# Turning the attention probabilities by VectorE's 32 by 32 blocks and SBUF to SBUF transfers in a decoder megakernel

## What is computed

```python
q = rope(x @ Wq)        # 8 batches, 32 heads, 128 rows, 128
k = rope(ctx @ Wk)      # 8 heads
v = ctx @ Wv            # 8 heads
p = softmax(q @ k.T / sqrt(128) + mask)   # causal in layer 0, the given mask in layer 1
x = layernorm(x + (p @ v) @ Wo)
```

## Time and profile before

| | us |
|---|---|
| three executions | 2656.85, 2662.54, 2663.20 |
| their median | 2662.54 |
| span of the profiled execution (first to last instruction) | 2658.3 |
| busy in it: TensorE, VectorE, ScalarE, GpSimd | 2568.0, 1579.7, 1074.0, 714.2 |

### The profile page before, as it was taken

The page is one execution under the profiler, slowest core; times in us unless marked ns, Lnnn a source line. Parts: engine busy times, 40 slices in busy tenths (PEclk is TensorE's granted clock), DMA queues, the critical chain, the costliest instruction groups (busy, mean ns, idle before and its releaser), DMA issues.

```text
span 2658.3 us, 39957 instructions
## 1 busy us (share of the span) xinstructions
PE 2568.0 (97%) x15160; PEld 1681.2 (63%) x15160; DVE 1579.7 (59%) x2953; ACT 1074.0 (40%) x3270; POOL 714.2 (27%) x695
## 2 busy tenths in 40 slices
PE   8989999999999899999999999999999989999998
PEld 7855676766665676566676766656775554556664
DVE  3487666766646666776666766454556644334465
ACT  0013444444454466244444444613555412324440
POOL 1037334444321100463334443122211221000002
PEclk9999999999999999999999999999999999999999
DMA  8541001111001100101011110010000020000000
GB/s 175 98 129 54 10 35 40 40 40 36 5 16 40 48 2 2 60 32 36 7 38 40 40 40 17 1 72 33 1 2 29 22 72 28 13 0 25 13 1 32
DMA packets 55359, 94.86 MB, mean 36 GB/s; under 512 B 31456, under 2 KB 40096, under 8 KB 49024
## 3 DMA queue, kind: packets, MB, share of 16 engines
q1 hardware_dynamic: 55168, 92.30, 11.7%
HBM read 83.89 MB, written 8.39 MB: 35 GB/s over the span
## 4 chain that ended last, share of the span: by engine, by line
PE 87%; DVE 8%; ACT 2%; POOL 2%; issue 1%; DMA 0%; DVEq 0%; SPq 0%; POOLq 0%
PE banks L687 12%; PE banks L775 11%; PE banks L759 4%; PE banks L834 4%; PE banks L803 4%; PE banks L668 4%; PE banks L303 3%; PE banks L655 3%; PE banks L2028 3%; PE banks L1450 3%; PE banks L1977 3%; PE banks L2282 2%; PE banks L2005 2%; PE banks L2316 2%; PE banks L813 2%; PE banks L2044 2%
## 5 line engine op out<-in xcount | busy, mean ns | idle before, releaser
L161 POOL TENSOR_TENSOR norm_spread<-norm_mv,const 128x1 f32<-128x1 f32 x96 | 20.7, 216 | 1128.2 <-DVE norm_mv L157 1128.2
L880 ACT ACTIVATE E_x<-S_x,sm_x 128x128 f32<-128x128 f32 x512 | 199.2, 390 | 261.8 <-DVE sm_x L1052 260.4
L1112 POOL TENSOR_TENSOR QT<-QT,const 128x512 f32<-128x512 f32 x128 | 171.1, 1337 | 469.6 <-DVE turned L938 469.6
L687 PE MATMUL banks<-xT,weights 128*128 128x512 f32 x512 | 236.1, 595 | 5.8 <-POOL weights L1107 5.8
L1016 DVE TENSOR_TENSOR x<-banks,x 128x256 f32<-128x256 f32 (+1 forms) x288 | 147.3, 511 | 123.7 <-PE banks L775 119.7
L775 PE MATMUL banks<-weights,OT 128*128 128x256 f32 x768 | 189.4, 379 | 0.0
L1114 POOL TENSOR_TENSOR QT<-QT,turned 128x512 f32<-128x512 f32 x128 | 168.9, 1320 | 10.0
L2415 ACT ACTIVATE E_s<-banks,top_s 128x128 f32<-128x128 f32 x512 | 139.3, 383 | 79.2 <-DVE top_s L2512 79.2
L887 ACT ACTIVATE OT<-banks 128x512 f32<-128x512 f32 x128 | 76.5, 597 | 227.1 <-PE banks L834 227.1
L687 PEld LDWEIGHTS banks<-xT,weights 128*128 128x128 f32 x512 | 95.0, 191 | 114.1 <-issue 106.4
L775 PEld LDWEIGHTS banks<-weights,OT 128*128 128x128 f32 x768 | 141.8, 190 | 38.3 <-DVE x L1016 11.7
(11 more groups left out here) (315 smaller groups left out, 5185.0 us busy)
## 6 DMA issues: line engine op xcount, KB each, us to landing
weights<-in_L_xwq SPq DMA_DIRECT2D x16, 1024.0 KB, 4.9
weights<-in_L_xwo SPq DMA_DIRECT2D x16, 1024.0 KB, 4.9
weights<-in_L_xwk SPq DMA_DIRECT2D x16, 256.0 KB, 5.0
weights<-in_L_xwv SPq DMA_DIRECT2D x16, 256.0 KB, 2.6
weights<-in_L_ffn_W_base SPq DMA_DIRECT2D x3, 1024.0 KB, 5.0
weights<-in_L_xwq SPq DMA_DIRECT2D x4, 768.0 KB, 6.8
weights<-in_L_xwo SPq DMA_DIRECT2D x4, 768.0 KB, 6.3
xT<-in_xT SPq DMA_DIRECT2D x4, 512.0 KB, 9.7
```

Source lines behind the costliest of these rows:

```text
L687: mm = PE.matmul(to, left[:, k, head], moving, start=name in ("P1", "P2", "P4", "P5") and k == 0, stop=k == 1, skip_group_check=name in (" ...
L880: ins = AC.activation(e[:, j, :], s[:, j, :], ACT.Exp, bias=sm[:, 0, j:j + 1], scale=1.0, accum_out=sm[:, 1, j:j + 1])
L1112: PO.tensor_tensor(four(to), four(to), spread(cos128, 4), ALU.mult).then_inc(*pool_step.one())
```

## The change

For the first 62 units of each of the two stages (`direct = units - 2`), the four transposes on TensorE and ScalarE's copy of their result are gone. ScalarE writes and scales E in another order: 16 blocks of 32 columns, block j of head h at place (j, h). VectorE turns E in 32 by 32 blocks into a new tile `blocks` (`turn_blocks`), in the step after the unit's own, right after the maxima. SyncE then starts sixteen transfers (`move`): 32 partitions by 128 columns each, quarter i of the partitions of `blocks` to quarter j of those of PT. TensorE waits for all sixteen and reads PT in the order (h, i, c). E has two tiles instead of three. The last two units of each stage go the old way. The weights wq and wo are loaded in four transfers each instead of one, and SyncE's loads are placed between the units' moves, two groups ahead for wk, wq and wv.

```diff
 def load_cross(stage, free):
...
-            for name, here in (("wk", xwk_in), ("wv", xwv_in), ("wq", xwq_in)):
+            for name, here in (("wk", xwk_in), ("wv", xwv_in)):
                 SP.dma_start(views[name], dram[f"{layer}_x{name}"][0]).then_inc(*here.one())
-            SP.dma_start(views["wo"][0], dram[f"{layer}_xwo"][0]).then_inc(*xwo_in[0].one())
+            for k in range(KC):
+                SP.dma_start(views["wq"][:, k, :], dram[f"{layer}_xwq"][0, :, k, :]).then_inc(*xwq_in.one())
+            for k in range(4):
+                SP.dma_start(views["wo"][0][:, k, :], dram[f"{layer}_xwo"][0, :, k, :]).then_inc(*xwo_in[0].one())
...
+            direct = units - 2
...
-                E = [sbuf(f"E{n}_x{stage}", [P, 4, P], scope) for n in range(3)]
+                E = [sbuf(f"E{n}_x{stage}", [P, 4, P], scope) for n in range(2)]
+                blocks = [sbuf(f"blocks{n}_x{stage}", [P, 4, P], scope) for n in range(2)]
...
+                def flat(t):
+                    return t[:, :, :].rearrange("p a n -> p (a n)")
+
+                def head_of(e, h, u):
+
+                    if u < direct:
+                        return flat(e).rearrange("p (j h c) -> p h j c", j=4, h=4)[:, h, :, :]
+                    return e[:, h, :]
...
+                def turned_rows(u):
+
+                    t = PT[u % 2]
+                    return flat(t).rearrange("p (i h c) -> p h i c", i=4, h=4) if u < direct else t[:, :, :]
...
+                    def move(u):
+
+                        SP.wait_ge(*x_blocks(u + 1))
+                        if u >= 2:
+                            SP.wait_ge(*x_mix(u - 1))
+                        for j in range(4):
+                            for i in range(4):
+                                SP.dma_start(flat(PT[u % 2])[32 * j:32 * j + 32, rows_of(i)], flat(blocks[u % 2])[32 * i:32 * i + 32, rows_of(j)]).then_inc(*x_pt_in[u % 2].one())
+
+                    load_keys(1)
+                    load_queries(1, range(KC))
+                    load_values(1)
+                    load_out(1, range(4))
+                    for u in range(direct):
+                        g, b = divmod(u, B)
+                        move(u)
+                        if b == 2 and g + 2 < G8:
+                            load_keys(g + 2)
+                        if b == 3 and g + 2 < G8:
+                            load_queries(g + 2, range(KC))
+                        if b in (4, 5) and 2 <= g + 1 < G8:
+                            load_out(g + 1, range(2 * (b - 4), 2 * (b - 3)))
+                        if b == 7 and g + 2 < G8:
+                            load_values(g + 2)
...
-                        if 2 <= step < units + 2:
+                        if direct + 2 <= step < units + 2:
                             u = step - 2
                             PE.wait_ge(*x_prob(u + 1))
-                            if u:
-                                PE.wait_ge(*x_pt(u))
+                            if u > direct:
+                                PE.wait_ge(*x_pt(u - direct))
                             for h in range(4):
-                                mm = PE.transpose(psum[4][:, rows_of(h)], E[u % 3][:, h, :], ident)
+                                mm = PE.transpose(psum[4][:, rows_of(h)], E[u % 2][:, h, :], ident)
...
-                            PE.wait_ge(*x_pt(u + 1))
+                            if u < direct:
+                                PE.wait_ge(*x_pt_in[u % 2](16 * (u // 2 + 1)))
+                            else:
+                                PE.wait_ge(*x_pt(u - direct + 1))
...
-                            PE.matmul(psum[5][:, :], V[g % 2][:, b, :], PT[u % 2][:, :, :], start=True, stop=True).then_inc(*x_mix.one())
+                            PE.matmul(psum[5][:, :], V[g % 2][:, b, :], turned_rows(u), start=True, stop=True).then_inc(*x_mix.one())
...
-                        if u >= 3:
-                            AC.wait_ge(*x_pturn(u - 2))
+                        if u >= 2:
+                            AC.wait_ge(*x_blocks(u - 1))
...
+                    def turn_blocks(u):
+                        DV.wait_ge(*x_prob(u + 1))
+                        if u >= 2:
+                            DV.wait_ge(*x_pt_in[u % 2](16 * (u // 2)))
+                        DV.transpose(flat(blocks[u % 2]), flat(E[u % 2])).then_inc(*x_blocks.one())
...
                             DV.tensor_reduce(sm[:, 0, :], s[:, :, :], AX.X, ALU.max, negate=True).then_inc(*x_top.one())
+                        if 1 <= step <= direct:
+                            turn_blocks(step - 1)
```

More of the change, by code:

```diff
@@ L488, in build @@
         x_mix, x_ot, x_out, x_sum = (signal(f"cross_{n}") for n in ("mixed", "ot_here", "out_product", "x_added"))
+        x_blocks = signal("cross_blocks_turned")
+        x_pt_in = [signal(f"cross_pt_in{n}", 16) for n in range(2)]
         def load_cross(stage, free):
@@ L626, in wo_here @@
                 def wo_here(g):
-                    return xwo_in[g % 2].sem, wo_base[g % 2] + 16 * (g // 2 + 1)
-                def sp_cross():
[L630 to L637, removed]
+                    return xwo_in[g % 2].sem, wo_base[g % 2] + 64 * (g // 2 + 1)
@@ new lines, in flat, with scores_of @@
+                def flat(t):
[4 more added lines that the diff above has]
+                    return e[:, h, :]
+                def scores_of(s, h, u):
+                    return s[:, h, :].rearrange("p (j c) -> p j c", j=4) if u < direct else s[:, h, :]
+                def turned_rows(u):
+                    t = PT[u % 2]
+                    return flat(t).rearrange("p (i h c) -> p h i c", i=4, h=4) if u < direct else t[:, :, :]
@@ new lines, in sp_cross, with load_keys, load_queries, load_values @@
+                def sp_cross():
+                    def load_keys(g):
+                        SP.wait_ge(*x_keys(2 * g))
+                        SP.dma_start(views["wk"], dram[f"{layer}_xwk"][g]).then_inc(*xwk_in.one())
+                    def load_queries(g, ks):
+                        SP.wait_ge(*x_query(4 * g))
+                        for k in ks:
+                            SP.dma_start(wq[:, k, :], dram[f"{layer}_xwq"][g, :, k, :]).then_inc(*xwq_in.one())
+                    def load_values(g):
+                        SP.wait_ge(*xv_mm(2 * g))
+                        SP.dma_start(views["wv"], dram[f"{layer}_xwv"][g]).then_inc(*xwv_in.one())
+                    def load_out(g, ks):
@@ L638, in sp_cross @@
                         if g == 1:
                             SP.wait_ge(*before.added)
-                        if g >= 2:
+                        else:
                             SP.wait_ge(*x_out(outs_to(B * (g - 1) - 1)))
-                        if g:
-                            SP.dma_start(wo[g % 2], dram[f"{layer}_xwo"][g]).then_inc(*xwo_in[g % 2].one())
+                        for k in ks:
+                            SP.dma_start(wo[g % 2][:, k, :], dram[f"{layer}_xwo"][g, :, k, :]).then_inc(*xwo_in[g % 2].one())
@@ L909, in act_cross @@
                             continue
-                        if step < units + 2 and not jobs_at(step, 0):
+                        if direct + 2 <= step < units + 2:
                             turned_copy(step - 2)
@@ L1044, in dve_cross @@
                             u = step
-                            s, e, sm = S[u % 2], E[u % 3], small[u % 3]
+                            s, sm = S[u % 2], small[u % 3]
                             DV.wait_ge(*x_score(u + 1))
```

25 lines of the change are left out of this document (10 added, 15 removed).

## The result

| | before | changed |
|---|---|---|
| executions, us | 2656.85 to 2663.20 | 2891.68 to 2894.52 |
| median | 2662.02 | **2892.71** |
| span of the profiled one | 2658.3 | 2892.2 |
| granted clock, mean | 0.993 | 0.962 |

The ratio is 1.0869, 95% interval 1.0854 to 1.0885: 230.7 us slower, where +40 was forecast and the range ended at 2790. The direction was right, the size was not.

A forecast was written before the change was run, and what follows sets the result against it. The prediction took TensorE's stream as the bound. A stage: -27.3 (transposes) + 4 (VectorE) + 36 (waits for transfers) + 7 (clock) = +20, so +40 over two stages: 2702 us, range 2630 to 2790.

The forecast's parts named there:

- What SyncE gets: SyncE's queue: sixteen transfers a unit at 0.475 us a start, 7.6 us a unit; TensorE waits 36 us a stage.
- The upper bound of 0.67: SyncE's queue: the most one start-to-start interval of the new transfers could take, in us; the lower bound was 0.375.
- rival 1: SyncE's queue: an issue is dearer than 0.475; 2758 us at 0.53, about 2900 at 0.67; chance 0.22.
- In the middle that fits on average: Middle groups: SyncE's moves and weights take 65 us of a group of 76.8; uneven steps still cost 2.7 a group.
- the 8 us of VectorE: VectorE's block turn delays OT's sums, making TensorE wait 0.7 us in six groups a stage: +4 us a stage.
- The end: Stage end, units 54 to 61: SyncE needs 60.8 us against TensorE's 42.8, so TensorE waits 18 us, plus half a microsecond.
- The landing: SyncE's transfers: 2.0 us from issue to landing, so a unit's last piece lands 9.05 us after its first issue may start.
- What goes: TensorE's stream: four transposes of E gone in 124 units at 0.44 us each, -54.6 us, 27.3 a stage.
- rival 3: VectorE becomes the bound: a 0.7 us wait in every step, 43 a stage instead of 4, 2780 us; chance 0.05.
- The clock: TensorE's granted clock drops after 2 us waits in the middle: +7 us a stage; nothing at the stage's end.
- What is cheap: the weights' issue order: SyncE's weight loads: reordering their issue was taken as cheap, each still being loaded a group ahead.
- Rival 2: SyncE's queue: at 0.375 us an issue the transfers mostly hide and the kernel gets faster, 2637 us; chance 0.23.

The follow-up runs named there:

- experiment 1: Kernel before, plus runs of 32 back-to-back transfer starts of each form after its output is stored; only starts read: 0.632 us apart between SBUF tiles, 0.461 loading from HBM.
- Experiment 8: Changed kernel with only units 0 to 53 of each stage going the new way, the last ten the old way: 2823.98 us, ratio 1.0607.
- The unturned version: Changed kernel with one 128x512 transfer a unit instead of sixteen and no block turn by VectorE (output differs): 2619.72 us, ratio 0.9845 to before.
- the fast version: By its 77.5 us groups, apparently the changed kernel with one 128x512 transfer a unit instead of sixteen (output differs): 2623.07 us, ratio 0.9856 to before.
- two versions whose intervals overlap: Changed kernel with one 128x512 transfer a unit, with VectorE's block turn 2623.07 us, without it 2619.72 us.
- experiments 2 and 5: Changed kernel with eight 32x256 transfers a unit: 2655.67 us; 5 also starts the wq loads ahead of the group's fourth unit's transfers: 2622.88 us.
- experiment 9: Changed kernel with all sixteen transfers, wq loads started ahead of the group's fourth unit's transfers: 2904.28 us, ratio 1.0916 to before.
- experiment 10: Changed kernel regrouping through HBM (four stores, one load a unit), wq loads ahead of the fourth unit's transfers: 2620.63 us, ratio 0.9849 to before.
- experiment 2: Changed kernel with eight transfers of 32x256 a unit instead of sixteen of 32x128 (output differs): 2655.67 us, ratio 0.9968 to before.

## Why the prediction was wrong

- **The step that failed is in "What SyncE gets": "The new ones are two-dimensional, so I take 0.475."** A start between two SBUF tiles takes 0.633 from start to start, alone (experiment 1) and in the kernel. I chose by the number of dimensions, the only thing that the rows let me compare. For a two-dimensional transfer of 32x128 or 128x128, the memories at the ends make the difference (0.46 or 0.63, experiment 1), and no row of the trace had two SBUF ends. The upper bound of 0.67 held the value, and rival 1 named the cause and, for 0.67, the time ("about 2900"); it had 0.22, and the range left that end out.
- **With it fell "In the middle that fits on average".** A group needs 8 x 16 x 0.633 = 81.0 for the moves and ten weights' starts, about 5.2: 86.2 us, where TensorE has 76.8. SyncE's sum passes TensorE's at (76.8 - 5.2) / 128 = 0.56 a start; above that SyncE sets the pace, and each 0.01 of a start costs 1.3 us a group. Two smaller things come on top. 36 of the 1984 starts took over 0.9 us (1.4 in the mean), 0.8 more than usual, 1.9 a group. And SyncE waited 19.2 us for blocks in the five groups from 360 to 820, 3.8 a group; that a late product makes late scores, and these late blocks, is my reading. Together 91.9, measured 90.5 to 92.4; the forecast's working gives 81.4. That working, unit by unit, with 0.633 for every start, a landing of 1.8 and the 8 us of VectorE gives +214 for both stages, and some +203 with the weights' starts at their measured 0.52; measured 233.9 on the spans. That the long starts make up the difference is argued, not shown.
- **The end**: forecast 7.6 us a step, measured 73.9 / 7 = 10.6; the starts alone are 16 x 0.633 = 10.1. The step was right in kind (SyncE's pace), short by the same term. Experiment 8 puts it at 34 us a stage, the forecast at 18.5 less the 3.5 of the transposes.
- **The landing**, 2.0 in the forecast, was 1.8: near enough.
- **What goes**: -54.6 was too much. The unturned version has neither the sixteen starts nor VectorE's turn and gains 42.3, or 0.34 a unit. In six of a middle group's eight steps the gain is the forecast's 0.43 or 0.44 (13.36 to 12.93, 9.27 to 8.83); in two it is 0.27 and 0.09 (9.27 to 8.99, 4.78 to 4.69). With VectorE's turn a middle group goes from 80.3 to 77.5, the -2.8 that the forecast has in -3.5 + 0.7, but by chance: the parts are -3.0 and +0.2, the latter nearly all in the group's first step (12.07 to 12.25). What else is missing lies in a stage's first measured group (1.9 us less in stage 1, 1.5 more in the second attention, where 3.5 less was due) and in its last seven steps (2.2 less, where 3.1 was due); why, no run shows. The Trainium skill (VectorE: DVE Perf Modes, The three transpose paths) gives 390 ns for a bf16 turn of 128x128 on TensorE, from which the prediction estimated 193 us; the rows decided, and the runs agree with them: 42 us for 496 turns, 85 ns each.
- **VectorE**: 8 us forecast, 3.4 measured between two versions whose intervals overlap; rival 3 is out.
- **The clock**: it fell, but as forecast for the end it costs nothing where SyncE sets the pace. In the middle TensorE was busy 71.09 us of 80 for work that takes 67.8 at the pace of the fast version (80 x 77.5 / 91.4): 3.3 us slower, beside 8.9 idle, and both end at the same landing. That is read from one window, and no run separates it, but SyncE's budget above bounds it: a slower TensorE can lengthen a middle group only through SyncE's waits for blocks, 3.8 us. The 7 us a stage were no term of their own.
- **What I did not foresee**: the order of SyncE's queue. "What is cheap: the weights' issue order" is wrong by 33 us between experiments 2 and 5. In the full change, where SyncE is the bound, the same move gains nothing (experiment 9).
- Rival 2, faster, was right in what it would take. The Trainium skill (DMA: Bandwidth & Descriptors, Issuing engines are not separate DMA queues) says that the sequencer's time to start a transfer is usually small beside the transfer. For one transfer of this case it is 0.59 against 1.8 to landing. For sixteen that depend on nothing but the queue it is 10.1 against 1.8, and the queue is what ends last. With one start, eight, or four and one it is hidden, and the change is worth about 40 us.

## What to carry to other kernels

Count the starts of transfers as instructions of the engine that issues them, each with a duration measured for the pair of memories at its ends, and set their sum against the length of a step before anything else: here 10.1 us a unit against 9.6. If the sum does not fit, regroup the transfer so that it needs fewer starts (through HBM four stores and a load did the work of sixteen); a second queue helps only if its engine has nothing behind the starts that others wait for. And look at what is queued behind the new starts: a weight load that was early before can become late, and its harm shows on other engines.

## What the runs showed of the hardware

- A start of a two-dimensional transfer takes 0.59 us (0.633 from start to start) between two SBUF tiles and 0.42 (0.46) with HBM at one end, within 0.02 the same for 32 and 128 partitions and, for SBUF, for 512 and 2048 bytes a partition. With more dimensions the HBM case can take 0.63 (line 267 of the earlier trace rows). In the change the first start of a unit took 0.51 in the median; in experiment 1 the first of a run took 0.47 to 0.60 between SBUF tiles.
- SyncE's and ScalarE's queues each keep that pace when both start at once (0.64 each).
- A transfer's landing grows little with its size: 1.8 us for 16 KB, 2.6 for 256 KB between SBUF tiles (line 2586 of experiment 1), 2.7 for 256 KB from HBM (experiment 10).
- VectorE's product of two SBUF tiles went from 0.69 to 1.45 and 1.66 us beside GpSimd's sums (experiment 2), while its scaling of a PSUM bank stayed at 0.68. The Trainium skill (SBUF — State Buffer, SBUF: two separate sides) says that the two engines share a port pair as an exclusive lock, which a VectorE instruction with two SBUF inputs takes against a GpSimd instruction that reads SBUF; the rows agree with it.
